# A graph network with one zero-filled bias matrix: Pool's fill copies described as the even and then the odd rows of 10 KB

## What is computed

```python
x = _layernorm(x + _L0_gnn_ref(x, edge_index, edge_weight, L0_gnn_weight, L0_gnn_bias), axis=-1)
x = _layernorm(x + _L1_gnn_ref(x, edge_index, edge_type_2, ...), axis=-1)
x = _layernorm(x + _L2_gnn_ref(x, edge_index, L2_gnn_W, L2_gnn_b), axis=-1)
x = _layernorm(x + _L3_gnn_ref(x, edge_index, edge_attr_8, ...), axis=-1)
```

```python
logits = jnp.einsum('ehd,ehd->eh', q[rows] * scale, k[cols]) + att_bias
...
y = jax.ops.segment_sum(att[:, :, None] * v[cols], rows, num_segments=n)
```

## Time and profile before

| | us |
|---|---|
| median of 3 runs | 1253.46 |
| the three runs | 1247.01, 1256.37, 1253.46 |
| the profiled execution, its time | 1259.67 |
| its span | 1257.9 |
| busy in the span: TensorE (PE) | 1181.3 (94%) |
| VectorE (DVE) | 851.3 (68%) |
| ScalarE (ACT) | 437.1 (35%) |
| GpSimd (POOL) | 307.6 (24%) |

### The profile page before, as it was taken

One profiled execution on the slowest core, in us unless ns is written; L12 is line 12 of the kernel. 1 busy time (PEld: TensorE's weight loads), 2 busy tenths in 40 slices (PEclk: granted clock), 3 DMA queues, 4 the chain that ended last, 5 costly groups with the idle time before them and its releaser, 6 DMA issues.

```text
span 1257.9 us, 21464 instructions
## 1 busy us (share of the span) xinstructions
PE 1181.3 (94%) x8083; PEld 540.5 (43%) x8084; DVE 851.3 (68%) x1330; ACT 437.1 (35%) x586; POOL 307.6 (24%) x220
## 2 busy tenths in 40 slices
PE   6987879999999999999999999999999899999997
PEld 2333334323344334345445454455333365555553
DVE  7575657544434555553368875575999889899997
ACT  2444546512122222112311002216553255444454
POOL 2000000000010133344655655545556000000000
PEclk9988989999999999999999999999999899999999
DMA  8567867598799789753122213112223376565653
GB/s 327 209 217 247 297 224 269 151 407 305 243 363 307 257 285 314 278 165 109 2 35 35 50 19 69 2 3 33 34 33 67 139 235 231 202 220 187 213 186 112
DMA packets 64325, 222.73 MB, mean 177 GB/s; under 512 B 31138, under 2 KB 36002, under 8 KB 48272
## 3 DMA queue, kind: packets, MB, share of 16 engines
q1 hardware_dynamic: 34706, 156.38, 35.8%
q0 software_dynamic: 25184, 53.10, 16.7%
q10 hardware_dynamic: 4350, 12.07, 2.8%
HBM read 198.92 MB, written 59.92 MB: 206 GB/s over the span
## 4 chain that ended last, share of the span: by engine, by line
PE 69%; DVE 11%; issue 7%; DMA 7%; ACT 3%; SPq 2%; DVEq 1%; ACTq 0%
PE PS L1853 26%; PE PS L1802 10%; PE PS L1727 6%; PE PS L1657 5%; PE PS L2098 4%; PE PS L2085 4%; DMA R<-R 4%; DVE R L1172 4%; DVE R L1209 4%; PE PS L1675 3%; PE PS L1967 2%; PE PS L2144 2%; PE PS L1889 1%; PE PS L1773 1%; DMA W<-in_basis_s 1%
## 5 line engine op out<-in xcount | busy, mean ns | idle before, releaser
L812 POOL DMA_INDIRECT bias_d<-R x160 | 271.0, 1694 | 331.3 <-DMA bias_d<-R 220.5
L1853 PE MATMUL PS<-R 128*128 128x512 f16 x1300 | 298.1, 381 | 0.0
L1853 PEld LDWEIGHTS PS<-R 128*128 128x128 f16 x1300 | 120.5, 98 | 180.6 <-issue 49.7
L1727 PE MATMUL PS<-R,XX 125*128 125x512 f16 (+2 forms) x612 | 134.7, 354 | 15.3 <-ACT R L1400 6.8
L1613 ACT ACTIVATE R<-PS 128x1024 f32<-128x1024 f32 (+1 forms) x100 | 106.2, 1087 | 109.6 <-PE PS L2085 77.9
L1802 PE MATMUL PS<-W,XX 128*128 128x512 f16 x600 | 136.0, 386 | 5.1 <-DVE R L1010 2.7
L926 DVE TENSOR_SCALAR R<-W,R 125x1250 f16<-125x1250 f16 x160 | 89.4, 606 | 53.7 <-PE PS L1727 39.4
L1172 DVE CUSTOM_DVE_ANT_0 R<-PS,R 128x1250 f16<-128x1250 f32 x80 | 116.8, 1459 | 5.5 <-PE PS L2021 2.9
L2098 PE MATMUL PS<-R 128*32 128x256 f32 (+1 forms) x1600 | 102.5, 391 | 5.2 <-DVE R L1209 5.2
L2085 PE MATMUL PS<-R 128*128 128x256 f16 (+3 forms) x800 | 99.6, 275 | 5.4 <-ACT R L1613 2.2
L779 POOL DMA_DIRECT2D bias_d<-bias_d x39 | 21.6, 556 | 324.0 <-PE PS L1727 164.2
(11 more groups left out here) (231 smaller groups left out, 1411.0 us busy)
## 6 DMA issues: line engine op xcount, KB each, us to landing
bias_d<-bias_d POOLq DMA_DIRECT2D x39, 1280.0 KB, 9.0
R<-in_basis_s SPq DMA_DIRECT2D x32, 1024.0 KB, 6.9
W<-in_basis_s SPq DMA_DIRECT2D x28, 1024.0 KB, 6.1
W<-bias_d SPq DMA_DIRECT2D x27, 1024.0 KB, 4.9
XX<-bias_d SPq DMA_DIRECT2D x13, 1024.0 KB, 4.9
R<-key_d SPq DMA_DIRECT2D x20, 500.0 KB, 4.0
R<-R SPq DMA_DIRECT2D x120, 80.0 KB, 5.9
W<-bias_d SPq DMA_DIRECT2D x7, 904.0 KB, 4.6
```

Source lines behind the costliest of these rows:

```text
L812: pool.indirect_dma_start(bias_d, bass.IndirectOffsetOnAxis(ap=idx[:, c:c + 1], axis=0), attr[:, c, :], None, bounds_check=DUMP + GC * P - ...
L1727: ins = T.matmul(mm_out(3 * (j % 2) + b, p1 - p0), own[0:EC, bass.ds(c, 1), :, :].rearrange("p c m w -> p (c m w)"), hots(p0, p1), start=f ...
L1853: ins = T.matmul(mm_out(SUM_BANK(s, i), D), lhs, rhs, start=n == 0, stop=n == len(terms) - 1)
```

## The change

Each of the 39 DRAM-to-DRAM copies moves the same bytes to the same place; only the order in which its access pattern names the 128 rows differs: first the 64 even rows, then the 64 odd ones, on both sides. Two rows named one after the other so never touch.

```diff
                 else:
-                    pool.dma_start(cells[n], cells[0]).then_inc(zero_out, 16)
+                    pool.dma_start(cells[n].rearrange("(a b) e -> b a e", b=2),
+                                   cells[0].rearrange("(a b) e -> b a e", b=2)).then_inc(zero_out, 16)
```

## The result

The changed kernel takes 1299.73 us, the median of 4 runs (1288.62 to 1301.99); the kernel before took 1250.24 in the same comparison. The ratio is 1.0365 (95% interval 1.0314 to 1.0417); the two medians alone give 1.0396. The prediction was 1300, slower. Of its terms only the weights came out by their own working. The first stores came out in size and by another way; the build went the other way and was 36.8 us off; the eleven copies that were to cost nothing cost 24.2 us, and a load behind the build that was not in the sum cost 9.3. That these errors nearly cancel is luck.

A forecast was written before the change was run, and what follows sets the result against it. TensorE, busy 94% of the span, was taken as the bound, so its waits on DMAs beside copies decide. Stores 5, build 20 and weights 22 sum to +47 on the median 1253.46, giving 1300 us; range 1240 to 1375.

The forecast's parts named there:

- the weights: PE's wait before layer 1: weights' loads take turns with the 28th copy's packets and land late, +22 us.
- The first stores: ACT's first stores beside the first two copies: two more groups held at issue, +5 us, ends 0 and +14.
- the build: The 40 windows beside 24 copies: R<-R lands in 6.6 us, windows take 4.95 us, +20 us (-18 to +55).
- the eleven: Last eleven copies: 54 us on engines with two, hidden by VectorE's work before Pool's first indirect DMA, cost nothing.
- the 28th copy's landing: Sign of right: Pool's copies take 25 us or more to land even alone, the 28th some 30 us.
- q0 shows 128 full packets a copy: Sign of right, on Pool's queue: q0 shows some 128 packets a copy.
- The windows: Sign of right, in the build: the windows take near 5 us each.
- Pool's first indirect DMA waits for the copies: Sign of wrong: Pool's first indirect DMA is held by the copies; the forecast had VectorE's work hide them.
- ACT's waits for R<-R are gone: Sign of wrong, in the build: R<-R lands under 5 us beside copies and ACT's waits for it vanish.
- Where the packets go: Each copy's 128 packets are dealt by the leading dimension, 64 to each of two engines, successive copies on different ones.
- Four in 6.6 us are three in 4.95: Build: four transfers on the way, landing in 6.6 us, give a window's three R<-R every 4.95 us.
- two engines, but small packets give way: Rival, 13%: R<-R lands in 4.1 us; build -18, stores nothing, weights +10; -8 in all, 1245 us.

## Why the sum was right and its parts were not

The terms, against the profiled execution that the prediction counted from (spans, us):

| term | predicted | changed kernel | alone |
|---|---|---|---|
| first stores | +5 | +3.0 (first window 72.2 to 75.2) | |
| build | +20 | -16.8 | -17.3 (152.6, build's copies only) |
| behind the build, without the weights | not seen | +9.3 | +11.7 (same run) |
| weights | +22 | +20.3 (PE's wait 22.1 against 1.75) | +19.4 (27th and 28th only) |
| the eleven | 0 | +24.2 (against the run with them as before) | 0 (ratio 0.9995) |
| sum | +47 | +40.0; the spans differ by 39.4 | |

The medians differ by 49.5 and not 39.4, since the profiled execution of before lies some 10 us above its median. Most of that is in its build, where the runs that kept the 40 KB copies range from 160.2 to 169.9. Against the other four of these the changed kernel's build gains 7 to 15 us and not 16.8, and its sum comes nearer to the 49.5. That +47 met +40 in one execution, and 1300 the median, is luck: the build was 36.8 us off one way, the eleven and the stretch behind the build 33.5 the other.

Of the prediction's own signs, the late weights and the 28th copy's landing (31.5 us) came as for "right", and q0 shows 128 full packets a copy, among 1024. The windows did not come: 153.1 / 39 = 3.9 us each and not 5. One sign of being wrong came in full, that Pool's first indirect DMA waits for the copies, and half of another: ACT's waits for R<-R are gone, though R<-R lands in 7.5 us and not under 5.

**Where the packets go** was right: two engines, others for the next copy. The two copies that travel alone keep a quarter of the engines busy, and the counts of entries fit. A copy has 1024 with two groups, 512 with four (128, and 384 of the smallest), 128 with sixteen, always 16 engines times the number of packets on one. The Trainium skill, page "DMA: Bandwidth & Descriptors", section "Why a DMA increments its semaphore by 16 and not by 1", has the rule on the largest number of engines up to 16 that divides the slowest dimension, and on consecutive engines from a moving cursor; the runs with 2, 4 and 16 groups agree. That the two engines are neighbours no run here shows.

**The step on the build failed: "Four in 6.6 us are three in 4.95".** The landing itself was well sized: the median is 7.5 us in the changed kernel's page, and was to be 6.6. But four transfers on the way were not a limit of the transfers. From 184 to 204 us the changed kernel's DMA view has this row:

```profile
R<-R SPq DMA_DIRECT2D x15, 80.0 KB, 9.9
```

That is 15 x 9.9 / 20 = 7.4 on the way at once, five windows in 20 us at a landing of 9.9, and ACT waits for none of them, because a place is needed again only 15.2 us after it was filled. The earlier trace rows shows 13 in 20 us at 6.2 us each, and they were late because SP issued them late (1.24 us an issue, 0.70 in the changed kernel). The prediction read a landing time as a pace without asking how old a transfer may become. Its rival "two engines, but small packets give way" had the build's size right (-18), though by an R<-R that lands in 4.1 us, which was 7.5, and the weights at +10 wrong.

**The step "Nothing: the eleven" failed**, in two of its numbers. It had the eleven issued at one go; Pool was held for 27.2 us after the second. And it gave the engines with two copies 128 x 0.42 = 54 us, with no turns for SP's loads, though the weights' term had counted just such turns; it is 0.71 us for each packet, 91 us in all. From the last issue, over at 406.7, to the first indirect DMA at 494.7 there are 88. The slack was judged rightly (15 us forecast, some 20 found). The turns alone would have stayed within it, as far as the run with the eleven alone shows: it has them and no hold, and costs nothing. No run takes the hold alone out of the changed kernel.

**The weights** came out by their own working: a copy's 64 packets in turns with loads that are waited for. **The first stores** came out in size only (+3.0 for +5). The prediction had two more groups of ACT's stores held at their issue, 2.2 us each. No group is held (1.33 to 1.60 us a group); what costs time is that the stores land later, ACT's 5.5 us.

**The load of the basis behind the build was not in the sum.** It starts beside the last copies of the build just as the weights' loads do beside the 28th, and the prediction looked for places where PE hangs on a DMA "while copies run", in the kernel before. There copies were over in 9 us; at 25 us and more each reaches into the next stage.

## What to carry to other kernels

In this kernel the leading dimension of a big copy and the size of its packets are two knobs: the first sets on how many engines it stands and how long it stays there, the second what each small transfer beside it pays and, on sixteen engines, how fast another queue can issue. Sixteen groups of 10 KB, which this change missed by one number, are faster than both kernels (1238.53 us, ratio 0.9914). Before a landing time is turned into a pace, look for how long its buffer may wait and whether the issuing queue keeps up.

## What the runs showed of the hardware that was not expected

- **Empty entries.** A copy that uses 2 of 16 engines adds 896 entries of next to no bytes, as many as 64 for each of the other 14 (that they lie so is not shown): under-512-B packets rise by 39 x 896 (and one), by 39 x 384 with four engines (31,138 to 46,114), by none with sixteen.
- **Pool's hold.** The copy that was issued last before the first hold, at 138.02, has this time to landing:

```profile
DMA to landing us min/median/max: 31.2/31.2/31.2
```

  It is issued by 138.91, lands by 170.1, and Pool goes on at 169.75: the hold ends about when what is under way has landed. An engine's entries for a copy are counted here as 64 and one for the semaphore's increment, which the packets do not show. The hold comes after 15 copies of 65 entries (975) twice in the changed kernel, once, in the build, in the runs that changed only the build's copies (31.67 us) or all but the last eleven (31.46 us), after 30 of 33 (990) with four groups, and never with 39 of 17 (663) or eleven of 65 (715). Without the one it is 960 in both cases. It costs most just ahead of a batch that is waited for. What it is that fills up is not shown.
- **SP's issues.** With 40 KB packets on all sixteen engines SP's issue of a small DMA takes 1.24 us in the mean and up to 4.4 in the kernel before; with 10 KB packets, or with 40 KB on two engines, mostly 0.6 (in the changed kernel up to 2.2). Why a big packet of another queue holds an issue stays open; the runs separate its conditions and not its cause.
